# Five right operands for six, the block input's split and W1's pieces near the slot's head

## What is computed

```python
B, M, D, H = 2048, 39, 16, 128
x0 = xk = x                                  # (B, M, D)
for W in (W0, W1):                           # (1, M * Hk, H); Hk is 39, then 128
    Wr = W.reshape(m, Hk, Hn)
    xk = jnp.einsum('bid,bjd,ijh->bhd', x0, xk, Wr)
    outs.append(xk)
return jnp.sum(jnp.concatenate(outs, axis=1), axis=-1)
```

## Time and profile before

| what | value |
|---|---|
| median of 3 runs | 580.67 us (578.86 to 581.48) |
| the profiled execution's own time | 579.92 us |
| its span, first to last instruction | 578.1 us |
| TensorE (PE) busy | 550.1 us, 95% |
| DVE, ACT, POOL busy | 472.1, 470.0, 480.9 us |
| moved by DMA | 163.78 MB, mean 283 GB/s |
| granted TensorE clock | 0.994 of full speed |

### The profile page before, as it was taken

How to read it: one execution, slowest core, us unless ns; L and a number is a source line. 1 busy time by engine, 2 the same in 40 slices (tenths; PEclk the granted TensorE clock), 3 DMA queues, 4 the chain that set the end, 5 groups by cost and what they waited for, 6 DMA issues and landing times.

```text
span 578.1 us, 10856 instructions
## 1 busy us (share of the span) xinstructions
PE 550.1 (95%) x3186; PEld 483.1 (84%) x3186; DVE 472.1 (82%) x816; ACT 470.0 (81%) x983; POOL 480.9 (83%) x407
## 2 busy tenths in 40 slices
PE   5788788999999999999999999999999999999998
PEld 3476677878888888988988998898889889889988
DVE  4688888888888898888889888888988888888740
ACT  4698888889888888888888888888888888888740
POOL 6998899899989888889988888898888899888800
PEclk9799999999999999999999999999999999999999
DMA  8999999999899989999999989999999989988210
GB/s 318 331 352 317 326 312 304 306 305 295 267 306 332 307 298 290 279 324 287 288 301 312 303 268 305 315 296 293 313 285 281 325 292 300 295 304 285 52 52 10
DMA packets 66489, 163.78 MB, mean 283 GB/s; under 512 B 10112, under 2 KB 18816, under 8 KB 66432
## 3 DMA queue, kind: packets, MB, share of 16 engines
q1 hardware_dynamic: 66432, 163.09, 88.0%
HBM read 139.98 MB, written 2.10 MB: 246 GB/s over the span
## 4 chain that ended last, share of the span: by engine, by line
PE 71%; ACT 10%; DMA 6%; issue 5%; POOL 4%; DVE 2%; SPq 1%; ACTq 0%; DVEq 0%; POOLq 0%
PE acc L397 12%; PE acc L399 11%; PE acc L398 11%; PE fin L448 6%; PE fin L449 6%; PE fin L450 6%; DMA outs<-w_dram 5%; PE pg L433 5%; PE pg L431 5%; PE pg L432 5%; ACT fh L510 4%; PE turn L409 4%; PE acc L392 2%; POOL fl L761 2%; ACT gh L552 1%
## 5 line engine op out<-in xcount | busy, mean ns | idle before, releaser
L761 POOL TENSOR_TENSOR fl<-fs,fh 128x512 fp32r<-128x512 f32 x192 | 249.7, 1304 | 42.8 <-ACT fh L510 40.1
L397 PE MATMUL acc<-fh,w0h 128*128 128x512 f32 x384 | 160.3, 417 | 15.3 <-ACT x L533 10.1
L756 POOL TENSOR_TENSOR fs<-xr,xs 128x512 f32<-128x512 f32 x128 | 163.0, 1295 | 0.9 <-DMA xr<-xb_dram 0.8
L647 DVE TENSOR_TENSOR fp<-xl,xr 128x512 f32<-128x512 f32 x192 | 133.5, 697 | 31.4 <-ACT xl L517 18.4
L399 PE MATMUL acc<-fl,w0h 128*128 128x512 f32 x384 | 151.9, 395 | 0.0
L398 PE MATMUL acc<-fh,w0l 128*128 128x512 f32 x384 | 151.5, 395 | 0.0
L651 DVE TENSOR_TENSOR fl<-fp,fh 128x512 fp32r<-128x512 f32 x192 | 131.9, 687 | 23.1 <-ACT fh L510 18.2
L510 ACT ACTIVATE fh<-fp 128x512 fp32r<-128x512 f32 x192 | 114.5, 596 | 36.3 <-PE acc L399 30.6
L666 DVE TENSOR_TENSOR gl<-pg,gh 128x320 fp32r<-128x320 f32 x252 | 117.0, 486 | 25.8 <-ACT gh L552 20.6
L510 ACT ACTIVATE fh<-fs 128x512 fp32r<-128x512 f32 x192 | 121.4, 632 | 10.8 <-PE acc L399 8.6
L552 ACT ACTIVATE gh<-pg 128x320 fp32r<-128x320 f32 x252 | 105.5, 439 | 18.4 <-PE pg L433 17.6
(11 more groups left out here) (67 smaller groups left out, 724.0 us busy)
## 6 DMA issues: line engine op xcount, KB each, us to landing
xr<-xb_dram SPq DMA_DIRECT2D x192, 512.0 KB, 5.7
xbd<-xdhl SPq DMA_DIRECT2D x256, 80.0 KB, 4.0
xs<-xa_dram SPq DMA_DIRECT2D x64, 256.0 KB, 4.1
xdr<-xd_dram SPq DMA_DIRECT2D x64, 160.0 KB, 3.9
xp<-xpairs_dram SPq DMA_DIRECT2D x32, 256.0 KB, 4.3
outs<-w_dram SPq DMA_DIRECT2D x9, 256.0 KB, 6.6
out_dram<-outs SPq DMA_DIRECT2D x7, 256.0 KB, 5.8
fs<-w0a_dram SPq DMA_DIRECT2D x1, 256.0 KB, 4.8
```

Of the source, the lines that this page charges most:

```text
L397: nc.tensor.matmul(acc[:, :], w0h[:, t, :], fh[:, t, :], start=t == 0, stop=False)
L647: nc.vector.tensor_tensor(f_at(t), xl[:, :], xr[:, gi % 2, t, :], ALU.mult).then_inc(prod_dve, 1)
L756: nc.gpsimd.tensor_tensor(f_at(t), xr[:, gi % 2, t, :], xs[:, gi % 2, :], ALU.mult)\
L761: nc.gpsimd.tensor_tensor(fl[:, t, :], f_at(t), fh[:, t, :], ALU.subtract).then_inc(low_pool, 1)
```

## The change

Four things change.

- The pairs are placed differently. The rows of a tile come from triples of fields (a, b, c): a is the left operand, b and c the right operands of tiles 0 and 2, and tile 1 is b * c, both factors taken from the right operands. So five right operands are loaded and not six, in parts of two, two and one. POOL's product 1 reads `xr` twice.
- `xdr` gets two buffers and two semaphores. SP loads the block input of group g + 3 at the slot's end, and ACT's `xd_split` moves from behind `turned_high` to ahead of `high(g + 1, 0)`.
- W1's raw pieces get a buffer of their own, `w1r`. SP issues `w1_load` at the head of its slot, where it stood at the end, and ACT's `w1_high_part` moves to right behind `high(g + 1, 0)`.
- SP waits for product 2 where it waited for product 0, and the start and `first_out` are reordered accordingly.

```diff
+PLACE = {0: 0, 2: 1, 3: 2, 4: 3, 5: 4}
+BOTH_RIGHT = 1
+NR = len(PLACE)
+PARTS = (slice(0, 2), slice(2, 4), slice(4, 5))
+PART_OF = {0: 0, BOTH_RIGHT: 0, 2: 0, 3: 1, 4: 1, 5: 2}
-        xr = sb("xr", [P, 2, NT, GC])
+        xr = sb("xr", [P, 2, NR, GC])
-        xdr = sb("xdr", [P, 2, NQ, MI])
+        xdr = sb("xdr", [P, 2, 2, NQ, MI])
+        w1r = sb("w1r", [P, NW, H])
...
             def w1_load(p):
                 if p:
                     sp.wait_ge(w1_ready, p)
                     sp.wait_ge(w1_ready_dve, p)
+                else:
+                    sp.wait_ge(w0_ready, 3)
                 sp.dma_start(w1_raw(p), w1[:, piece(p), :]).then_inc(w1_in, 16)
...
+                    if (first or second) and 0 <= g + 1 - W1_SLOT < PIECES:
+                        w1_load(g + 1 - W1_SLOT)
                     if more3:
-                        wait_product(sp, g + 1, 0)
                         wait_product(sp, g + 1, 4)
+                        wait_product(sp, g + 1, 2)
                         load_x(j, gi + 3)
                         load_right(j, gi + 3, 0)
                     blocks(g, gi, first)
...
-                    if not (last and gi + 1 >= CB):
-                        sp.wait_ge(xd_low, g + 2)
-                    if more2:
-                        load_xd(g + 2)
                     if more3:
                         wait_product(sp, g + 1, 3)
                         load_right(j, gi + 3, 1)
                     if more3:
                         wait_product(sp, g + 1, 5)
                         load_right(j, gi + 3, 2)
-                    if (first or second) and 0 <= g + 1 - W1_SLOT < PIECES:
-                        w1_load(g + 1 - W1_SLOT)
+                    if not (last and gi + 1 >= CB):
+                        sp.wait_ge(xd_low, g + 2)
+                    if more3:
+                        load_xd(g + 3)
...
+                    if more and g:
+                        xd_split(j, gi + 1, False)
                     if more:
                         high(g + 1, 0, False)
+                    if (first or second) and 0 <= g - W1_SLOT < PIECES:
+                        w1_high_part(g - W1_SLOT)
...
                     if prev:
                         turned_high(g - 1)
-                    if more:
-                        xd_split(j, gi + 1, first and gi == 0)
-                    if (first or second) and 0 <= g - W1_SLOT < PIECES:
-                        w1_high_part(g - W1_SLOT)
+                    if first and gi == 0:
+                        xd_split(0, 1, True)
...
             def product(j, gi, t, fresh):
                 g = CB * j + gi
-                if t == POOL_PROD[0]:
+                if t == BOTH_RIGHT:
+                    left, place = xr[:, gi % 2, PLACE[0], :], PLACE[2]
+                else:
                     pool.wait_ge(xs_in[gi % 2], 16 * nth(j, gi))
-                pool.wait_ge(xr_in[t // 2][gi % 2], 16 * nth(j, gi))
+                    left, place = xs[:, gi % 2, :], PLACE[t]
+                pool.wait_ge(xr_in[PART_OF[t]][gi % 2], 16 * nth(j, gi))
```

More of the change, by code:

```diff
@@ L21 @@
 TILES = NT + 1
-LOADED = range(NT)
+HALF = M // 3
+PLACE = {0: 0, 2: 1, 3: 2, 4: 3, 5: 4}
[3 more added lines that the diff above has]
+PART_OF = {0: 0, BOTH_RIGHT: 0, 2: 0, 3: 1, 4: 1, 5: 2}
+STARS = (3, 4, 5)
 LEFT = range(18, 30)
@@ L44 @@
 HIGH = (0, 1, 2, 4, 3, 5)
-NU = NT // 2
+NU = len(PARTS)
 W0_PART = 4
@@ L70, in pieces_before, with triples, point, labels @@
     return min(-(-row // NW), PIECES)
[L73 to L79, removed]
+def triples():
+    def point(x, i):
+        return HALF * (i % 3) + x % HALF
+    yield from ((point(x, 0), point(x, 1), point(x, 2)) for x in range(HALF))
+    for x in range(HALF):
+        for y in range(x + 1, HALF):
+            for i in range(3):
+                yield point(x, i), point(y, i), point((x + y) * (HALF + 1) // 2, i + 1)
+def labels():
+    system = list(triples())
+    whole = {k * len(system) // P for k in range(P)}
+    count = [0] * M
+    rows = []
+    for triple in (system[k] for k in sorted(whole)):
+        apex = min(triple, key=lambda v: (count[v], v))
+        count[apex] += 1
+        rows.append((apex, *(v for v in triple if v != apex)))
+    pairs = [(t[k], t[l]) for n, t in enumerate(system) if n not in whole
+             for k, l in ((0, 1), (0, 2), (1, 2))]
+    pairs += [(i, i) for i in range(M) if i not in LEFT]
+    cap = [len(STARS) * c for c in count]
+    held = {v: [] for v in range(M)}
     def settle(pair, tried):
@@ L98, in pair_slots @@
         assert settle(pair, set())
-    free = {v: [(t, m) for t in LOADED for m in range(v, P, M)] for v in cap}
-    return [(*free[v].pop(), v, i + j - v) for v, got in held.items() for i, j in sorted(got)]
+    out = []
+    for apex, b, c in rows:
+        out.append((apex, b, c, *(sum(held[apex].pop()) - apex for _ in STARS)))
+    return np.array(out)
+def pair_slots(of):
+    for m, row in enumerate(of.tolist()):
+        for t, k in PLACE.items():
+            yield t, m, row[0], row[1 + k]
+        yield BOTH_RIGHT, m, row[1 + PLACE[0]], row[1 + PLACE[2]]
 def left_rows(u):
@@ L152, in build @@
         w0a_raw = [fs[:, SBUF_F[4], :].rearrange("p (t h) -> p t h", h=H),
-                   xr[:, 1, NT - 1, :].rearrange("p (t h) -> p t h", h=H)]
+                   w1r[:, :, :]]
         w0b_raw = [outs_as_w, x1[:, :].rearrange("p (t h) -> p t h", h=H)]
@@ L170, in build @@
         sq_ready = sem("sq_ready")
-        xd_in = sem("xd_in")
+        xd_in = [sem("xd_in0"), sem("xd_in1")]
         xd_high = sem("xd_high")
@@ L201, in w1_raw @@
         def w1_raw(p):
-            rows = outs[:, :, :].rearrange("p a b -> p (a b)").rearrange("p (n h) -> p n h", h=H)
-            return rows[:, 0:piece(p).stop - piece(p).start, :]
+            return w1r[:, 0:piece(p).stop - piece(p).start, :]
         def tile_n(g, t):
@@ L271, in load_right @@
             def load_right(j, gi, u):
-                sp.dma_start(xr[:, gi % 2, 2 * u:2 * u + 2, :], xb[CB * j + gi][:, 2 * u:2 * u + 2, :])\
+                sp.dma_start(xr[:, gi % 2, PARTS[u], :], xb[CB * j + gi][:, PARTS[u], :])\
                   .then_inc(xr_in[u][gi % 2], 16)
@@ L278, in load_xd @@
             def load_xd(g):
-                sp.dma_start(xdr[:, :, :, :], xd[g]).then_inc(xd_in, 16)
+                sp.dma_start(xdr[:, g % 2, :, :, :], xd[g]).then_inc(xd_in[g % 2], 16)
             def w0a_load(k):
@@ L355, in _ @@
             load_right(0, 1, 0)
+            load_right(0, 1, 1)
+            load_right(0, 1, 2)
             load_xd(0)
-            load_right(0, 1, 1)
             sp.dma_start(idn[:, :], ident).then_inc(ident_in, 16)
-            sp.wait_ge(w0_ready, 3)
-            load_right(0, 1, 2)
-            wait_product(sp, 0, 0)
+            load_xd(1)
             wait_product(sp, 0, 4)
+            wait_product(sp, 0, 2)
             load_x(0, 2)
             load_right(0, 2, 0)
-            sp.wait_ge(xd_low, 1)
-            load_xd(1)
             wait_product(sp, 0, 3)
@@ L370, in _ @@
             load_right(0, 2, 2)
+            sp.wait_ge(xd_low, 1)
+            load_xd(2)
             chunk(0, True, False, False)
@@ L536, in xd_split @@
                 g = CB * j + gi
-                act.wait_ge(xd_in, 16 * (g + 1))
+                act.wait_ge(xd_in[gi % 2], 16 * nth(j, gi))
                 if not fresh:
                     act.wait_ge(xbd_in[gi % 2], 16 * (BQ // 2) * (nth(j, gi) - 1))
-                nc.scalar.activation(xdhl[:, gi % 2, :, :, 0, :], xdr[:, :, :, :], COPY).then_inc(xd_high, 1)
+                nc.scalar.activation(xdhl[:, gi % 2, :, :, 0, :], xdr[:, gi % 2, :, :, :], COPY).then_inc(xd_high, 1)
             def turned_high(g):
@@ L642, in product @@
                     dve.wait_ge(xl_ready, g + 1)
-                dve.wait_ge(xr_in[t // 2][gi % 2], 16 * nth(j, gi))
+                dve.wait_ge(xr_in[PART_OF[t]][gi % 2], 16 * nth(j, gi))
                 dg, dt = BEFORE_IN_F.get(t, (-1, t))
@@ L646, in product @@
                     wait_low(dve, g + dg, dt)
-                nc.vector.tensor_tensor(f_at(t), xl[:, :], xr[:, gi % 2, t, :], ALU.mult).then_inc(prod_dve, 1)
+                nc.vector.tensor_tensor(f_at(t), xl[:, :], xr[:, gi % 2, PLACE[t], :], ALU.mult).then_inc(prod_dve, 1)
             def low(g, t):
@@ L750, in product @@
                 g = CB * j + gi
-                if t == POOL_PROD[0]:
+                if t == BOTH_RIGHT:
+                    left, place = xr[:, gi % 2, PLACE[0], :], PLACE[2]
+                else:
                     pool.wait_ge(xs_in[gi % 2], 16 * nth(j, gi))
-                pool.wait_ge(xr_in[t // 2][gi % 2], 16 * nth(j, gi))
+                    left, place = xs[:, gi % 2, :], PLACE[t]
+                pool.wait_ge(xr_in[PART_OF[t]][gi % 2], 16 * nth(j, gi))
                 if not fresh:
                     wait_low(pool, g - 1, t)
```

(19 more changed lines are left out.)

## The result

The changed kernel takes 639.5 us (median of 4 runs, 637.96 to 640.74); before it was 580.03 us (median of 4, 578.86 to 581.48). The ratio is 1.1023, 95% interval 1.0983 to 1.1062. The direction was forecast, the size was not: +59.5 us against +29.3, and above the range's end of 628.

The account below looks back on a forecast made before the run. TensorE, busy 550.1 of 578.1 us, was taken to bound the kernel. Terms of +31.7 (W1 loop), -1.5 (early slots) and 0 (later slots) made +30.2 on 579.9, so 610 us, likelier range 595 to 628.

Parts of the forecast that it names:

- the bytes: Early slots: fewer loaded bytes and earlier loads against the split's new wait for copies, together -1.5 us (bounds -5 and +3).
- slots 6 to 15: Loop of SP's W1 wait, copies and ACT's split: laps of 12.6 us, 121.4 us against 89.7, +31.7 us.
- the later slots: Steady slots: ACT's idle 1.2 us a slot covers a late copy landing; 0 us, bounds -2 and +4.
- Landing of that copy: Loop's leg from the last block copy's issue to its landing: 3.0 us taken, not less than 2.0.
- Behind much the same burst: Grounds for the landing time: in a steady slot the last two copies took 2.8 to 2.9 us behind a similar burst.
- The first lap: Slot 6 splits 1.3 us in; its lap of 7.0 + 3.0 + 3.3 + 0.2 brings slot 7's split to 14.8.
- The other legs: Rest of a lap: ACT, POOL and DVE 7.0 us in even slots, 5.7 in odd; SP 3.0 us.
- it just fits: Slots 1 to 5: copies land 8.4 to 9.6 us after the slot's head, and ACT asks at 9.9 us.
- The clock rival: TensorE's clock falls in the long slots, slots of about 16 us, 637 us; chance 0.07 of costing over 15 us.
- The sign that I had named: In the trace after, TensorE's clock under 0.8 from 70 to 190 us would show the forecast wrong.
- The other rivals: Early slots: loop does not bind, 572 us, chance 0.08; or no change, 579 to 583 us, chance 0.03.
- the least sum of 11.0: Shortest lap of the loop that rows give: 5.9 + 3.0 + 2.0 + 0.1 = 11.0 us.

Follow-up runs that it names:

- Experiments 1: The changed kernel with the W1 load back at the end of SP's slot, all else as changed: 593.5 us, ratio 1.024.
- 6: The changed kernel with every move kept and a second raw buffer for W1, so SP's wait asks for the low part made one slot earlier: 585.7 us, ratio 1.0085.
- 7: The changed kernel with the block copies of slots 6 to 14 issued ahead of the W1 load and its wait, operands' loads behind: 594.8 us.
- Experiment 4: The changed kernel with the block copies of slots 6 to 14 right behind the W1 load, ahead of left operand and right part: 611.5 us.
- the third: The changed kernel, but in slots 6 to 14 SP waits until the block copies have landed before it issues the next loads: 634.4 us.
- 2: The changed kernel with ACT's block split back behind the turned copy, the W1 load staying at SP's head: 597.9 us.
- 8: The changed kernel with W1's load back at SP's slot end, ACT's block split and W1's high part back behind the turned copy: 578.5 us, ratio 0.9947.
- 9: Kernel 8 with W1's high part early, near ACT's head, its load at the end of SP's slot: 591.2 us, ratio 1.0185.
- The tenth kernel: Kernel 8 with ACT's block split moved near its head: 580.5 us, ratio 0.9991.
- the eleventh: The tenth kernel with the block copies ahead of the operands' loads in every slot: 581.3 us, ratio 0.9987.

## Why the prediction was wrong in size

The mechanism was right: SP's wait for the low part of W1, the copies behind it, ACT's split behind them, and W1's high part behind the split. Experiments 1, 6 and 7 show it from three sides. What failed is the size of one leg, the copies' landing. By the prediction's own steps, with the difference of the two spans (60.8 us) cut at ACT's rows that open slots 6 and 16 (62.33 and 152.00 before; 65.42 and 208.87 after):

| step | forecast | measured |
|---|---|---|
| "the bytes" and slots 0 to 5 | -1.5 | +3.1 |
| slots 6 to 15 | +31.7 | +53.8 |
| "the later slots" and the end | 0 | +3.9 |

- **The step that failed is "Landing of that copy".** I took 3.0 us and bounded it at 4.0, "as the queues have time to drain in a long slot". The critical chain of the changed kernel has the last copy's landing of slots 6 to 14:

```profile
78.53 5.42 DMA xbd<-xdhl
...
92.72 5.94 DMA xbd<-xdhl
...
108.88 5.29 DMA xbd<-xdhl
...
122.94 5.60 DMA xbd<-xdhl
...
138.76 5.98 DMA xbd<-xdhl
...
153.53 5.46 DMA xbd<-xdhl
...
169.21 4.88 DMA xbd<-xdhl
...
182.86 5.67 DMA xbd<-xdhl
...
198.75 4.62 DMA xbd<-xdhl
```

  That is 5.4 us on average, in a stretch whose DMA engines are busy for 56% of the time. The queue may drain in the slot, but what counts is the burst ahead of the copies, and that moves with them: 1.05 MB issued in the 1.3 us before. Experiment 4 shows it (2.1 to 2.8 us in slot 7 with 0.26 MB ahead). Eight laps of 14.9 us instead of 12.6 are 18.6 us of the 22.1 that are missing in this row of the table, and the landing alone, 2.4 us over the forecast in each, makes 19.4 (other legs were a little shorter).
- The rows were there to read: the earlier trace rows has a maximum of 6.8 us, and I leaned on the steady slot's 2.8 instead of asking for a slot of the same kind. "Behind much the same burst" was a misreading. In that steady slot no piece of W1 is loaded, and SP stood still for 0.8 us between the right part and the copies:

```profile
305.24 0.43 SPq L272 DMA_DIRECT2D xr<-xb_dram  x1
306.51 2.41 SPq L303 DMA_DIRECT2D xbd<-xdhl  x4
```

  In slot 10 of the kernel before, whose timeline I used, the copies follow the right part at once, and the last one lands 5.6 us after its issue, with the next loads right behind:

```profile
DMA to landing us min/median/max: 4.2/4.7/5.6
```

- The first lap is most of the rest: slot 6's split started 2.95 us into the slot and not 1.3, since it already waited 1.71 us for copies, and its lap took 15.7 us. From the last split to slot 16 it was 5.4 us, with 5.8 forecast.
- The other legs were right: 5.5 us in odd slots and 7.0 in even ones on ACT, POOL and DVE (98.74 to 105.72), where I had 5.7 and 7.0, and 3.2 us on SP, where I had 3.0. I had costed the first by POOL's rows; the chain runs over DVE's, which I had called nearly the same, and SP's nine waits are for DVE's half. They are 9.3 us each, not "some 5", as the laps are longer.
- **"The bytes"** was wrong in sign. In slots 1 and 2 ACT's split waits 3.4 and 3.0 us for copies. Those of slot 0 landed in 2.8 to 3.7 us, and the slot was too short for them; those of slot 1 took 5.4 to 6.1 us, where "it just fits" was reckoned with 2.8 to 4 us, the same slip. How much of the 3.1 us is from these waits one trace doesn't tell: four kernels that are alike in slots 0 to 5 (the changed one, the third, fourth and seventh) open slot 6 on ACT at 65.42, 64.47, 67.90 and 64.61 us. Those with the split in its old place and the copies where they were (2, 8 and 9) open it at 61.93, 64.45 and 62.49 us, on average 2.6 us sooner, and that is what the split's place seems to cost here. The gain that I looked for is real, 2 to 3 us, for fewer bytes and the second buffer together, and shows only where the moves are undone (experiment 8).
- **"The later slots".** Forecast 0, bounds -2 and +4, measured +3.9, of which +2.6 lie between FULL of slot 17 and of slot 63 (388.70 us against 386.12). The tenth kernel, with the split in the same place, has 385.8 us there, so its place alone doesn't show this cost. What does in the changed kernel was not found. The four timed executions of that kernel differ by 2.8 us, and the profiled one is the slowest, so part of it can be this spread.
- **The clock rival.** It was given 0.07 for a price above 15 us. The sign that I had named was a clock below 0.8 between 70 and 190 us; it was 0.82 over all of that and 0.79 from 72 to 144 us. The clock did fall in the laps: 0.50 from 103 to 107 us, after TensorE had worked 0.8 of the 4 us before, 1.00 from 111 to 115, 0.53 from 115 to 119. The Trainium skill (TensorE: Matmul & The Clock Gate, "HAM oscillation — how this bites in real kernels") tells of a clock that falls again with each wait for a DMA; these rows agree. But its price is next to nothing here. The chain through the laps has long TensorE pieces in two of them only, some 2 us each (89.14 to 91.12 and 149.95 to 151.93 us), and there SP issues the copies 0.05 us after the right part, as in the other laps. ACT's row that opens a slot waited for TensorE once, 2.32 us in slot 10, and its split waited 5.09 us for copies all the same. No run took the clock away by itself. One reading of mine was wrong: the clock did not come back "at once as work arrived". In the earlier trace rows it stood at 0.50 for 6 us in which TensorE worked 5.77.
- The other rivals fell: the loop binds, and a lap is 3.9 us over the least sum of 11.0.

## What to carry to other kernels

- Before a wait is moved to the head of an in-order queue, ask when in the slot its condition is made, and what stands behind it that this same slot or the next needs. Here a load with a slot to spare was put ahead of copies with none, and its wait closed a loop over SP, ACT and DVE. A second buffer, so that the wait asks for the slot before, removes the loop and keeps the place.
- Price a transfer's landing from one that stands behind the same burst, not from the median of its kind or from a quiet stretch; a lightly used DMA does not make it short.
- A load and its first use are moved together or not at all: W1's high part early with the load late cost 12.6 us, more than ACT's waits before.

## What the runs showed that I had not expected

- In slot 7, four copies of 80 KB landed in 4.5 to 5.9 us behind 1.05 MB, in 4.2 to 4.6 us behind the same with nothing following, and in 2.1 to 2.8 us behind 0.26 MB with everything following. The bytes ahead weigh more than those behind, and the average load (56%) did not tell it.
- ACT waits 21.5 us for copies in the tenth kernel and 2.0 us in the eleventh, and their ratios are 0.9991 and 0.9987. But its waits for W1 pieces rise from 0.6 to 10.7 us, so one wait was traded for another.
